# Routing tokens to experts partly inside the last batch of attention, with a table of expert and rank in place of a table of tiles

## The reference

```python
logits = x @ router_weight.T + router_bias            # 2048 tokens x 16 experts
top_val, top_idx = jax.lax.top_k(logits, TOP_K)       # TOP_K = 4
top_val = jax.nn.softmax(top_val, axis=-1)
router_scores = jnp.zeros_like(logits).at[jnp.arange(T)[:, None], top_idx].set(top_val)
gate_up = jnp.einsum('th,ehd->etd', x, gate_up_proj) + gate_up_proj_bias[:, None, :]
gate, up = gate_up[..., ::2], gate_up[..., 1::2]
gate = jnp.minimum(gate, LIMIT)
up = jnp.clip(up, -LIMIT, LIMIT)
glu = gate * jax.nn.sigmoid(gate * ALPHA)
out = jnp.einsum('etd,edh->eth', (up + 1.0) * glu, down_proj) + down_proj_bias[:, None, :]
out = (out * router_scores.T[:, :, None]).sum(axis=0)
```

## Time and profile before

| | us |
|---|---|
| median of 3 runs (lowest to highest) | 1603.31 (1599.92 to 1605.49) |
| the profiled execution | 1600.59 |
| its span in the profile | 1598.8 |
| PE busy | 1456.5 (91%) |
| DVE busy | 971.5 (61%) |
| ACT busy | 723.2 (45%) |
| POOL busy | 839.9 (53%) |
| from the end of attention to the first instruction of experts | 768.87 to 827.75 |

### The profile page before, as it was taken

The page is one execution under the profiler, slowest core; times in us unless marked ns, Lnnn a source line. Parts: engine busy times, 40 slices in busy tenths (PEclk is TensorE's granted clock), DMA queues, the critical chain, the costliest instruction groups (busy, mean ns, idle before and its releaser), DMA issues. The chain is left out here.

```text
span 1598.8 us, 28732 instructions
## 1 busy us (share of the span) xinstructions
PE 1456.5 (91%) x7582; PEld 1031.8 (65%) x7583; DVE 971.5 (61%) x1389; ACT 723.2 (45%) x1348; POOL 839.9 (53%) x681
## 2 busy tenths in 40 slices
PE   6999999799999999998269999999999999999990
PEld 5878887444444444442257887777777877877770
DVE  2324344778887888886765555555555555555554
ACT  4212222278777778775223434424434443444223
POOL 4425333555666765632415536666666666486322
PEclk9999999799999999999579999999999999999996
DMA  6201022564557547530724445655556565473326
GB/s 212 72 14 49 13 49 54 80 89 72 99 113 123 109 84 132 89 64 30 275 75 121 118 92 151 160 151 155 151 151 158 148 161 151 110 191 80 59 54 223
DMA packets 92658, 179.04 MB, mean 112 GB/s; under 512 B 17032, under 2 KB 19848, under 8 KB 91944
## 3 DMA queue, kind: packets, MB, share of 16 engines
q1 hardware_dynamic: 72888, 132.76, 32.8%
q0 software_dynamic: 18544, 44.84, 14.2%
q10 hardware_dynamic: 1152, 0.52, 0.2%
HBM read 115.03 MB, written 33.46 MB: 93 GB/s over the span
## 5 line engine op out<-in xcount | busy, mean ns | idle before, releaser
L896 DVE TENSOR_REDUCE stage<-ps_a 128x2 f32<-128x1024 f32 x256 | 300.3, 1218 | 80.2 <-PE ps_a L1204 79.6
L705 ACT ACTIVATE probs<-ps_b 128x512 f32<-128x512 f32 x512 | 278.0, 595 | 54.4 <-PE ps_b L1219 52.0
L1785 POOL TENSOR_TENSOR we_split<-we_raw,we_split 128x512 f32 (+1 forms) x192 | 250.5, 1543 | 97.3 <-ACT we_split L1776 95.2
L2070 PE MATMUL ps_y<-we_split,hT 128*128 x912 | 231.8, 403 | 4.3 <-DVE hT L2001 3.4
L2070 PE MATMUL ps_g<-we_split,xT 128*128 x912 | 230.2, 401 | 5.0 <-issue 4.3
L2070 PE MATMUL ps_u<-we_split,xT 128*128 x912 | 231.6, 403 | 0.0
L2070 PEld LDWEIGHTS ps_g<-we_split,xT 128*128 128x128 f32 x912 | 171.8, 190 | 52.9 <-issue 12.9
L2070 PEld LDWEIGHTS ps_y<-we_split,hT 128*128 128x128 f32 x912 | 166.2, 189 | 41.8 <-issue 7.2
L2070 PEld LDWEIGHTS ps_u<-we_split,xT 128*128 128x128 f32 x912 | 166.3, 189 | 34.8
L1936 ACT ACTIVATE hT<-ps_h 128x512 fp32r<-128x512 f32 x76 | 45.3, 597 | 296.5 <-PE ps_h L2051 240.3
L1886 POOL DMA_INDIRECT scratch_acc<-x_keep,to_rows x76 | 121.2, 1595 | 109.7 <-issue 51.6
(11 more groups left out here) (254 smaller groups left out, 2213.8 us busy)
## 6 DMA issues: line engine op xcount, KB each, us to landing
we_raw<-in_w_expert SPq DMA_DIRECT2D x192, 256.0 KB
stack<-xT_raw SPq DMA_DIRECT2D x192, 128.0 KB, 5.4
we_bias<-in_b_expert SPq DMA_DIRECT2D x16, 768.0 KB, 4.0
stage<-in_w SPq DMA_DIRECT2D x5, 1024.0 KB, 4.9
xT_raw<-in_xT SPq DMA_DIRECT2D x4, 1024.0 KB, 6.4
x_tok<-in_x POOLq DMA_DIRECT2D x16, 256.0 KB, 3.1
scratch_acc<-x_keep SPq DMA_DIRECT2D x1, 4096.0 KB, 18.0
acc_sb<-scratch_acc SPq DMA_DIRECT2D x8, 512.0 KB, 6.6
```

The costliest lines, as they stand in the source:

```text
L705: nc.scalar.activation(probs[:, n % 3, h], src[:], ACT.Exp, scale=DH ** -0.5).then_inc(b_kept, 1)
L896: nc.vector.tensor_reduce(out[:, :, i, k % NC], ps_a[i][:], AX.X, ALU.max, negate=True).then_inc(a_kept[i], 1)
L1785: nc.gpsimd.tensor_tensor(lo, W["raw"][:, k, c], hi, ALU.subtract).then_inc(W["lo"], 1)
L2070: mm = nc.tensor.matmul(out[:], left[:, a, c], w[:, bass.ds(par, 1), k, b, c].squeeze(1), start=(n == 0), stop=(n == len(passes) - 1))
```

## The change

It does five things.

1. In the last batch of attention the routing begins, in groups of four token tiles: groups 0 and 1 (tiles 0 to 7) in steps 0 to 6, group 2 (tiles 8 to 11) behind the step loop. DVE runs `top_experts`, `chosen_experts` and `rank_slots` of each, PE adds up the ranks in steps 3, 5 and 11 (`rank_tokens`), ACT keeps them (`keep_rank`) and takes the exponentials (`raise_shares`). POOL makes the one-hot tables of tiles 0 to 11 (`mark_tile`): 0 to 7 before `finish_heads(6)`, 8 and 9 before the power of batch 6, 10 and 11 before the last power. PE spreads them at the end (`spread_tile`).
2. A token's place is its expert and rank (`PLACES` = 16 x 16 columns of 128), which needs no count of tiles. `experts` finds a tile's column in a table `place`.
3. A token's weights are stored behind its row in `x2` (544 in place of 512 numbers a row) and come with the gather; ACT picks them out (`keep_weight`).
4. `route` only handles group 3 (tiles 12 to 15), and works on the tables of tiles with experts over partitions.
5. `make_head_rows` moves ahead of the last `reduces`; expert 1's load and two thirds of POOL's cut of expert 0's weights move from `route` to the start of `experts`.

```diff
@@ gpsimd, attention @@
+                if b == B - 1:
+                    pool.wait_ge(b_made, USE["exp", STEPS * b - 1, 3] + 1)
+                    for t in range(8):
+                        mark_tile(nc.gpsimd, pool, R, K, t, in_tiles[t], of_tiles[t])
                 if b >= 1:
                     finish_heads(b - 1)
...
+            for t in range(8, 10):
+                mark_tile(nc.gpsimd, pool, R, K, t, in_tiles[t], of_tiles[t])
             pool.wait_ge(y2_moments, B - 1)
             nc.gpsimd.tensor_tensor(rstd2[:], mean_var2[:, :, 1], minus_half2[:], ALU.pow).then_inc(y2_rstd, 1)
             for o in range(2):
+                if o == 1:
+                    for t in range(10, EARLY_TILES):
+                        mark_tile(nc.gpsimd, pool, R, K, t, in_tiles[t], of_tiles[t])
@@ vector, attention @@
             for n in range(N):
                 b, s = n // STEPS, n % STEPS
+                if b == B - 1 and s == 7:
+                    make_head_rows()
                 if n + LEAD < N:
                     reduces(n + LEAD)
...
+                if b == B - 1 and s in (0, 2):
+                    if s == 0:
...
+                        set_choices(nc, dve, R, K)
+                        number_tokens(nc, dve, R)
+                    dve.wait_ge(b_kept, USE["logits", s + 1] + 1)
+                    top_experts(nc, dve, R, K, s // 2, s // 2)
+                if b == B - 1 and s in (1, 3):
+                    chosen_experts(nc, dve, R, K, s // 2, s // 2)
+                if b == B - 1 and s in (5, 6):
+                    dve.wait_ge(b_kept, USE["rank", s - 5] + 1)
+                    rank_slots(nc, dve, R, K, s - 5, s - 5, K["rank"][:, (s - 5) % 2])
+            dve.wait_ge(b_kept, USE["logits", 5] + 1)
+            top_experts(nc, dve, R, K, 2, 2)
+            chosen_experts(nc, dve, R, K, 2, 2)
             invert_spread(0)
             invert_spread(1)
             moments(B - 2)
...
             add_spread(0)
+            dve.wait_ge(b_kept, USE["rank", 2] + 1)
+            rank_slots(nc, dve, R, K, 2, 2, K["rank"][:, 0])
             dve.wait_ge(y2_rstd, B - 1)
             for o in range(2):
                 last_norm(B - 2, o, x2_made)
...
             invert_spread(2)
+            share_weights(nc, dve, R, K, 0, 3)
             invert_spread(3)
@@ tensor, attention, behind the step loop @@
             turn_x2(NT - 2)
+            for t in range(0, 2):
+                spread_tile(nc, pe, R, table, t, in_tiles[t], of_tiles[t])
             logits(B - 1, (0,))
+            for t in range(2, 9):
+                spread_tile(nc, pe, R, table, t, in_tiles[t], of_tiles[t])
             turn_x2(NT - 1)
+            for t in range(9, EARLY_TILES):
+                spread_tile(nc, pe, R, table, t, in_tiles[t], of_tiles[t])
             logits(B - 1, (1,))
@@ route: new helper functions @@
+def rank_slots(nc, dve, R, K, g, at, rank):
...
+    chain(R, dve, nc.vector.tensor_tensor(K["picked"].rearrange("p (t k) e -> p t k e", k=K_TOP), chosen, rank, ALU.mult))
+    chain(R, dve, nc.vector.tensor_reduce(K["slot"], K["picked"], AX.X, ALU.add))
+    chain(R, dve, nc.vector.tensor_copy(K["slot_i"], K["slot"]))
...
+def mark_tile(compute, engine, R, K, t, in_tile, of_tile, at=None):
...
+    if t % 4 == 0:
+        engine.wait_ge(R["slots_made"], t // 4 + 1)
...
+def spread_tile(nc, pe, R, table, t, in_tile, of_tile):
...
+    pe.wait_ge(R["marked"], 2 * t + 2)
...
+    for k in range(K_TOP):
+        mm = nc.tensor.matmul(columns, in_tile[:, k], of_tile[:, k], start=(t == 0 and k == 0),
+                              stop=(t == NT - 1 and k == K_TOP - 1), skip_group_check=True)
@@ route: what is left of it @@
-            load_weights(sp, A, W, 1)
+            store_weights(sp, S, R, K["weights"], LATE, 1)
+
             sp.wait_ge(dummy_stored, 32)
             sp.wait_ge(acc_stored, 16)
...
-            for k in range(3):
-                split_lo(nc, pool, W, 0, 0, k, range(KC))
+            pool.wait_ge(R["marked"], 2 * NT)
+            split_lo(nc, pool, W, 0, 0, 0, range(KC))
...
+            top_experts(nc, dve, R, K, LATE, 0)
+            set_choices(nc, dve, R, K)
+            chosen_experts(nc, dve, R, K, LATE, 0)
+            share_weights(nc, dve, R, K, LATE, 1)
...
+            rank_slots(nc, dve, R, K, LATE, 0, ps_r[:, 0:K_TOP * E_])
+            for t in range(4 * LATE, NT):
+                mark_tile(nc.vector, dve, R, K, t, in_tile[:, t % 4], of_tile[:, t % 4], 0)
@@ experts @@
+            load_weights(sp, A, W, 1)
             for e in range(2, E_):
...
+            for k in (UP, DOWN):
+                split_lo(nc, pool, W, 0, 0, k, range(KC))
```

More of the change, by code:

```diff
@@ new lines, in choice_buffers, with sb, chain @@
+def choice_buffers(nc, ctx):
+    def sb(name, shape, dt=F32):
+        return ctx.enter_context(nc.sbuf_tensor(f"late_{name}", shape, dt))[:]
+    views = {name: sb(name, (P, 1) + shape) for name, shape in CHOICE_SHAPES}
+    for name, shape in CHOICE_TEMPS:
+        views[name] = sb(name, (P,) + shape, U32 if name == "top_i" else I32 if name in ("slot_i", "digit_i") else F32)
+    views["hi"] = sb("hi", (P, 1, 4 * K_TOP, E_))
+    views["ones"] = sb("ones", (P, P))
+    return views
+def chain(R, dve, instruction):
+    R["done"][0] += 1
+    instruction.then_inc(R["step"], 1)
+    dve.wait_ge(R["step"], R["done"][0])
@@ new lines, in set_choices, with number_tokens, top_experts @@
+def set_choices(nc, dve, R, K):
+    nc.vector.memset(K["ones"], 1.0)
+    chain(R, dve, nc.vector.memset(K["again"], 1.0))
+    chain(R, dve, nc.vector.memset(K["again"][:, :, 0:1], 0.0))
+def number_tokens(nc, dve, R):
+    chain(R, dve, nc.vector.tensor_scalar(R["token1"][:], R["iota_f"][:, 0:NT], float(P), R["iota_p"][:, 0:1],
+                                          ALU.mult, ALU.add))
+    chain(R, dve, nc.vector.tensor_scalar(R["token1"][:], R["token1"][:], 1.0, None, ALU.add))
+def top_experts(nc, dve, R, K, g, at):
+    logits = R["logits"][:, 4 * g:4 * g + 4]
+    chain(R, dve, nc.vector.tensor_tensor(logits, logits, R["b"][:].unsqueeze(1).to_broadcast([P, 4, E_]), ALU.add))
+    for t in range(4):
+        last = nc.vector.max(K["top"][:, t], logits[:, t])
+    chain(R, dve, last)
+    for t in range(4):
+        nc.vector.max_index(K["top_i"][:, t], K["top"][:, t], logits[:, t])
+    chain(R, dve, nc.vector.tensor_tensor(K["gap"][:, at], logits, K["top"][:, :, 0:1].to_broadcast([P, 4, E_]),
+                                          ALU.subtract))
+    chain(R, dve, nc.vector.tensor_copy(K["top_f"].rearrange("p (t k) -> p t k", t=4), K["top_i"][:, :, 0:K_TOP]))
@@ L1527, in route @@
+def route(nc, A, S, x, G, W, R, ident, table):
+    LATE = 3
     with ExitStack() as ctx:
@@ L1630, in _ @@
-            dve.wait_ge(set_, 2)
-            chain(nc.vector.memset(again[:], 1.0))
-            nc.vector.memset(again[:, :, 0:1], 0.0)
-            for t in range(NT):
-                last = nc.vector.max(top[:, t], logits[:, t])
-            chain(last)
-            for t in range(NT):
-                last = nc.vector.max_index(top_i[:, t], top[:, t], logits[:, t])
-            nc.vector.tensor_tensor(gap[:], top[:, :, 0:K_TOP], top[:, :, 0:1].to_broadcast([P, NT, K_TOP]),
-                                    ALU.subtract).then_inc(gap_made, 1)
@@ L2242, in decoder_layer @@
+            G = tile_tables(nc, keep)
             W = weight_buffers(nc, keep)
-            route(nc, A, S, x, G, W, R)
-            experts(nc, A, S, x, G, W)
-        last_norm(nc, S, out)
+            route(nc, A, S, x, G, W, R, ident, table)
+        experts(nc, A, S, x, G, W)
+    last_norm(nc, S, out)
 def kernel(x, ctx_2048, mask_Bx1x2048_fk1, L0_attn_Wq, L0_attn_Wk, L0_attn_Wv, L0_attn_Wu, L0_attn_Wo,
```

440 lines of the change are left out of this document (251 added, 189 removed).

## The result

| | before | changed |
|---|---|---|
| median of 20 runs each (lowest to highest), us | 1600.7 (1592.88 to 1607.01) | 1607.03 (1602.02 to 1609.76) |
| ratio to before, 95% interval | | 1.0038 [1.0026, 1.005] |
| span in the profile, us | 1598.8 | 1604.2 |

The changed kernel is slower by 0.38%, 6.3 us by the medians and 5.4 us by the two spans. The prediction said 1600, no change or slightly faster, and gave slower 0.30. Where the 5.4 us come from can be read off by cutting both traces at the same five places: the start of the routing stage (SP's first load), the start of experts, the first and the last bias of the gate product (DVE, once a tile), and the end.

The account below looks back on a forecast made before the run. It took PE to bound the experts loop and DVE's chain the routing stage. Attention +27, routing -29.5 and experts +1 summed to -1.5 us, 1599.1 or 1601.8, taken as 1600; range 1587 to 1611.

Parts of the forecast that it names:

- the experts' loop: Loop over 76 tiles: ACT's added small operation and register loads hide in its waits for PE, 0 us.
- rival D: Experts loop slows: ACT makes PE wait 0.1 us a tile, 8 us over 76 tiles, 1608; chance 0.05.
- Steps 0 to 7: Attention's last batch: added routing work on DVE ends the last reduction 16 us later, at 739.5 to 740.5.
- The two port terms: Last batch: DVE operations held at the port shared with POOL, +3 us in step 1, +4 in step 6.
- From there to step 14: Last batch: DVE's and POOL's chain to `last_norm(6)` makes PE wait 10 us; step 14 moves by +23.4.
- The tail: End of attention: cold PE +2.4, small products and clock, +4 in all, 0.45 off; attention ends at +27.
- Rival C: Last batch: POOL's marks cost 3.6 ns a column, 9 us more before `last_norm(6)`, 1608; chance 0.25.
- Rival B: Attention loses far less: without port waits the chain reaches step 14 11 us earlier, 1588; chance 0.36.
- A: Whole kernel: attention's loss and the routing stage's gain come out even, 1595 to 1605; chance 0.34.
- The routing stage: Between attention and experts: 58.0 becomes 28.5 us, -29.5, with DMA the new limit and DVE about 25 us.
- Experts' start: Start of experts: expert 1's load now begins as the first gathers do, +1 us, at most 3.

Follow-up runs that it names:

- e1: The changed kernel with ACT's cut of the next expert's weights moved ahead of its two look-ups in the experts loop: 1597.26 us, ratio 0.9978.
- e3: The changed kernel with DVE's `rank_slots(2)` and POOL's marks of tiles 8 and 9 behind the norms and powers they stood ahead of: 1597.66 us.
- e7: The changed kernel with only `keep_weight` moved behind ACT's cut of weights, `aim_to` with its look-up staying ahead: 1598.72 us, ratio 0.9989.
- e6: e5 with the store of `acc` for token tiles 0 to 13 moved from the routing stage into attention: 1579.09 us, ratio 0.987.
- e8: e1 with expert 1's load started only when the first three gathers have landed: 1595.06 us, ratio 0.997.
- e9: The changed kernel with the edits of e1 and e3, the early `acc` store of e6 and the later load of e8: 1576.92 us, ratio 0.9841.
- e2: The kernel before with only ACT's look-ups and a small operation ahead of the cut added, gathered rows kept at 2048 bytes: 1608.13 us, ratio 1.0046.
- e4: The kernel before with only `make_head_rows` moved ahead of the last reductions: 1596.92 us, ratio 0.9975.
- e5: The changed kernel with the edits of e1 and e3 together: 1586.85 us, ratio 0.9913.

## Why the prediction was wrong

**The step that failed** is the experts' loop: "I take 0, hidden in ACT's waits for PE", and rival D at 0.05, with the argument that ACT waits 3 us a tile. It cost 8.1 us, more than the whole net loss; without it the changed kernel would be 1597.3 (e1). The 240 us of waits of the earlier trace rows are a sum over 76 tiles, and they lie in the tiles without a cut: 61 tiles wait 3.7 us or more ahead of `hT`, 15 not at all. With a cut ACT has 5.5 us more to do, goes from the cut straight into `hT`, and has no wait to give. The view to read was the timeline of one tile of each kind, beside the diff of ACT's body, where the two look-ups stand just ahead of the cut. D's size was right (0.1 us a tile on average, 8 us), but as a mean over tiles it hid where it would fall, and so its chance was set too low.

**Steps 0 to 7** were mis-sized: the last reduction ended at 734.6, +11.1 for +16. The two port terms were 3 and 4 us and came out at 0.4 and 2.4. That POOL operations hold small DVE operations is right, for the kinds that can be held: beside busy marks a copy took 1.14 us (741.48) and others 0.54 to 1.45, while the four best-of-16 took 0.41 us (736.98) against 0.40 in the quiet routing stage, and a reduction 0.59. The Trainium skill, "SBUF — State Buffer", section "Who interferes with whom", says that a DVE instruction with at most one SBUF input, outside the 2-port modes, doesn't contend with GpSimd; for these best-of-16 operations and reductions the trace agrees. But step 1's scan and copy stood beside POOL's norm of batch 5 and lost next to nothing, and the marks of tiles 0 to 3 took 6.4 us (724.30 to 730.68) for the 7.5 counted. PE stood 4.13 us before step 8, not 8.

**From there to step 14** the mechanism was as forecast: PE stands 8.93 us (10 forecast), released by DVE's norm, which waits for POOL's power behind two marks. `top_experts(2)` and `chosen_experts(2)` took 9.3 us for 7.5, and the marks 4.5 us for 5.7. Step 14 moved by 16.7 for 23.4. e3 shows that this wait was the order's and worth 9.4 us.

**The tail** was +5.7 where the terms gave 3.6, and the term that was off is the clock's. The forecast took 0.15 us for a small product with its weights, and 1.2 us back from a warm clock. At the granted clock of 1.00 the first eight take 0.13 us each (778.71); from 779.88 on the trace grants 0.50, after PE had stood no more than 0.72 us at a time since 769.6, and the 28 take 0.22 us each. So the last turn, whose input was ready at 783.7, went at 787.5. Changed kernel:

```profile
778.71 1.04 PE L1750 MATMUL table<-stack,in_tile_low 128*128 128x32 f32 x8
779.80 1.78 PE L1320 MATMUL ps_b<-rw,late 128*128 128x16 f32 x8
```

In e7, which differs in the loop alone, the clock fell at 779.93 too but the products had started earlier. The same eight router products (1.78 us above) and the 28 took:

```profile
777.38 1.04 PE L1320 MATMUL ps_b<-rw,late 128*128 128x16 f32 x8
778.26 4.73 PE L1750 MATMUL table<-stack,in_tile_low 128*128 128x64 f32 x28
```

At 0.22 us for those behind the fall, the ones ahead of it took about 0.12 each, by estimate. So the forecast's 0.15 was no underestimate at the full clock.

**Rival C** falls: a mark of 512 columns takes 1.05 us, not the 1.28 of the sum, let alone 3.6 ns a column (1.84 us). **Rival B** was half right: attention ended 4.6 us earlier than A had it, not 11.

**The routing stage** was right in length and in cause: -29.2 for -29.5, its last wait a DMA's, and e6 confirms what stood behind it. DVE, counted at 25 us, was done after 21.0, which the queue hid. **Experts' start** is +2.7 (1 forecast, at most 3). In the traces the first gather is issued 0.6 us later behind the stage's start, since ACT looks up a place first, its rows come 1.6 us later, which is the later load's (e8 takes it back), and the first gate product takes 0.4 us more. The last 1.5 us of the sum are the last product of the loop (3.07 us before, 4.60 changed), and they are the clock's: the granted clock is 1.00 all through it before and 0.63 on average in the changed kernel. Elsewhere it takes 3.05 or 3.06 us where the clock fell only behind it (e3, e8, e9), 4.55 to 4.61 where 0.50 was granted for a part of it (e2, e4, e5, e6), and 5.48 at 0.50 throughout (e1, e7), with no link to the edits. Why the clock falls where it does is open.

The forecast also counted 9.7 us a tile, which is the stretch from 836 to 1570 over 76; a tile takes 9.29 us, and the loop 707.8.

Added up, the terms other than the loop come to -2.6 us in the traces where -1.5 was forecast. That they came so near is luck in part: attention cost 4.6 us less than forecast, and the experts' start, the last product and the routing stage gave 3.5 of it back. The loop was the one that had no counterweight.

## What to carry to other kernels

A mean wait says nothing on the few iterations that are unlike the rest: before an instruction is counted as hidden, look at the fullest iteration of the loop, and at what stands directly behind the new instruction on its engine. A look-up whose value an operation needs can leave the engine idle ahead of it; put it behind the long operation, not before. When work moves into a stage whose engines wait for one another, place each piece behind what the others wait for: the same work cost 9.4 us less when it stood a few instructions later. And when a stage is cut in half, look at its DMA queue: what was hidden becomes its length.

## What the runs showed of the hardware

- A look-up by ACT's sequencer leaves no idle time while a long enough operation runs (0.71 us of `bw` in e7, the cut in e1), and shows as idle time "issue" behind small ones: 0.27 us ahead of `to_rows` in a tile with a cut, most often 0.51 or 0.84 us ahead of `from_rows` in others (e1). The two look-ups and a small operation ahead of the cut cost 8 us of 716.
- PE can lose more than it was late: behind the cut shown, PE began the product with `hT` 0.40 us after the product ahead of it (`ps_x`) in the changed kernel and 0.35 before, yet the next weight load came 0.52 us late for no wait that the trace names. These idle times of the gate product's weight loads sum up, from the first to the last bias, to 20.0 us in the changed kernel, 20.1 in e3 and 21.3 in e2, the slow loops, against 11.3 before, 12.1 in e7 and 13.9 in e1. Why a late `hT` does that is open; it wasn't tried.
- The granted clock sets the price of small products too: eight router products of 16 columns took 1.04 us at 1.00 (e7, 777.38) and 1.78 us at 0.50 (changed, 779.80); the twelve products that end the loop 3.07 us at 1.00 (before) and 5.48 us at 0.50 (e1).
- POOL's products in the marks, with both operands repeated along an axis, are quicker than those in `finish_heads`: 1.05 us for 512 columns against 1.26.
